# Attention's keys, queries and values fetched from ScalarE's instruction stream, keys in six pieces, values stored by head group

## The chip, the core and the metric

The kernel runs on one core of a Trainium2 chip. The core has five engines with an instruction stream each: TensorE (PE, matmuls; its weight loads are listed apart as PEld), VectorE (DVE), ScalarE (ACT), GpSimd (POOL) and SyncE (SP), which here issues nearly all transfers. All transfers, whoever issues them, run on the core's 16 DMA engines. The metric is the time of one execution on the device in microseconds (us); lower is better.

## What is computed

The reference applies two blocks to x of 2 x 2048 x 512 numbers. The change touches the attention of the first block only:

```python
h = _ada_ln(x, cond, Wln1, bln1)
q = heads(h @ Wq + bq)          # B=2, H=16 heads of HD=32, L=2048
k = heads(h @ Wk + bk)
v = heads(h @ Wv + bv)
scores = einsum('bhqd,bhkd->bhqk', q, k) / sqrt(HD)
attn = softmax(scores, axis=-1)
out = einsum('bhqk,bhkd->bhqd', attn, v)
x = x + out @ Wo + bo
# then LayerNorm and a 512-2048-512 MLP, then a graph attention over 20 nodes
```

## The kernel before

The program is written by hand, engine by engine, with semaphores; each engine runs its stream in order. It has these stages: queries, keys and values (0 to 376 us), attention (376 to 2026 us), output projection, MLP, graph attention.

**First stage.** Eight chunks of 512 rows (`ci`), twelve steps each (`j`). Steps 0 to 7 make queries and keys, steps 8 to 11 values. Each result goes to a tile (`st`, `vst`) and from there by SP to internal DRAM: queries and keys to `qk_d`, values to `v_d` as plain rows, [B * S, D] (lines 592 and 597). At chunk 4 SP also loads the first keys into `ks` (`sp_load_k`, L377, three transfers of 1 MB at steps 1, 3 and 5) and the first two query blocks into `qs` (`sp_load_q`, L384, three transfers of 256 KB each, at steps 6 and 7); at step 8 it loads the next chunk of x (L547). The keys need three copies because a product is made of the high and low parts of numbers, and the rows of `ks` and `qs` hold high, low and high part (32 rows each).

**Attention.** A group `w` is one batch and four heads, 8 in all; `w` has four units `v` (512 queries each), 32 in all (`NU`). A unit is eight pairs `f` (two key tiles of 128 each, `kt` 0 to 15). For a pair:
- PE makes eight maxima products (`pe_max`, L359) and eight score products (`pe_scores`, L621) in turn, then the value products of the pair before, four heads of two key tiles (`pe_values`, L633). The maxima run 82 products ahead of the scores, so they need the queries of unit v + 2 from the seventh product of pair 5 of unit v on, and the keys of the next `w` from pair 5 of its third unit on.
- Scores go to three PSUM banks in turn: `pe_scores` n waits for exponential n - 3.
- ACT does one exponential for each score (`act_exp`, L689, tile `pt` of 8 slots), and, once a unit after pair 0, copies the finished values (`act_values`, L695).
- DVE reduces the maxima (`dve_max`, L372).
- The sums over keys are split: GpSimd adds the tiles `kt` 3, 5, 7, 9, 11, 13, 14 itself (`pacc`, L777), and issues accumulating transfers of 1 MB for `kt` 1, 2, 4, 6, 8, 10, 12 into two accumulators (`accd`, L767 the first two, L763 the others), where each waits for the last one on its own accumulator: 1, 4, 8, 12 on one and 2, 6, 10 on the other. After pair 0 of the next unit PE adds up all parts with products by ones (`pe_sums`, L639, 32 products), the last eight of them over the accumulator that `kt` 12 finishes.
- SP, once a unit: folds the sums (L792), stores and loads their reciprocals (L798, L805), stores two rows made of the maxima (L337, `qs<-nmr`) and the finished values (L812); GpSimd multiplies by the reciprocals (L749) after `kt` 9.

SP's place for the fetches: the queries of v + 2 at pair 2 behind the folding of the sums; the keys of the next `w` in three pieces of 1 MB, at pair 6 of the first unit and pairs 4 and 7 of the second; the values of the next `w` (1 MB, rows of 512 bytes) at pair 7 of the third. All stand in one stream with the other transfers, so the times at which they are issued follow from those:

```python
if v + NCH - c < NU and (c, f) in ((0, 6), (1, 4), (1, 7)):
    sp.wait_ge(s_pad, 5)
    if w >= 2:
        sp.wait_ge(s_sc, 256 * (w - 1))
    sp_load_k(w, ((0, 6), (1, 4), (1, 7)).index((c, f)))
```

`s_pad` 5 is given when GpSimd has filled the spare rows of the second key buffer (L525, L528), at the start of the attention.

Of the kernel before, what the change touches and what calls it, by code (L numbers as in the profile page):

```python
# [7 lines left out]
F32 = mybir.dt.float32  # L8
# [6 lines left out]
B, S, D = 2, 2048, 512  # L15
H, HD = 16, 32
# [7 lines left out]
CH = 512  # L24
NCH = S // CH
# [4 lines left out]
NU = B * (H // 4) * NCH  # L30
# [117 lines left out]
def program(nc, a):  # L148
    pe, act, dve, pool, sp = nc.tensor, nc.scalar, nc.vector, nc.gpsimd, nc.sync
    qk_d = nc.dram_tensor("qk_d", [B, 4, D, S], F32, kind="Internal").ap()  # L150
    v_d = nc.dram_tensor("v_d", [B * S, D], F32, kind="Internal").ap()
    ao_d = nc.dram_tensor("ao_d", [NT, 128, D], F32, kind="Internal").ap()
    r_d = nc.dram_tensor("r_d", [2, 4, CH], F32, kind="Internal").ap()
    x2_d = nc.dram_tensor("x2_d", [B * S, D], F32, kind="Internal").ap()
# [10 lines left out]
    with ExitStack() as ctx:  # L165
# [34 lines left out]
        qsb = take("qs", [128, 3, 4, CH], F32R)  # L200
# [83 lines left out]
        def pe_early(step):  # L284

            if step == 64:
                return
            if step == 65:
                pe.wait_ge(s_nm, 1)
                pe.transpose(ps[0:16, 6, 0:128], nm[:, :], ident[:, :]).then_inc(s_nt, 1)  # L290
                return
            u = step - step // 64 * 2
            v, n = divmod(u, 64)
            hq, kc = divmod(n, 4)
            if n == 0:
                pe.wait_ge(s_qd[v], 48)
                pe.wait_ge(s_kd[0], 48)
            if u == 64:
                pe.wait_ge(s_nh, 2)
            if u >= 2:  # L300
                pe.wait_ge(s_mr, u - 1)
            pe.matmul(ps[:, 6 + u % 2, :], qsb[0:96, v, hq // 4, 128 * (hq % 4):128 * (hq % 4) + 128],
                      ksb[0][0:96, hq // 4, CH * kc:CH * kc + CH], start=True, stop=True).then_inc(s_mm, 1)
# [47 lines left out]
        def pe_max(u):  # L351
            v, n = divmod(u, 64)
            w = v // NCH
            hq, kc = divmod(n, 4)
            if n == 0:
                pe.wait_ge(s_qd[v % 3], 48 * (v // 3 + 1))
                pe.wait_ge(s_kd[w % 2], 48 * (w // 2 + 1))
            pe_bank_free(("max", u))
            pe.matmul(ps[:, ring.bank["max", u], :], qsb[0:96, v % 3, hq // 4, 128 * (hq % 4):128 * (hq % 4) + 128],  # L359
                      ksb[w % 2][0:96, hq // 4, CH * kc:CH * kc + CH], start=True, stop=True).then_inc(s_mm, 1)  # L360
# [11 lines left out]
            dve.tensor_reduce(nmp[:, n // 4, n % 4:n % 4 + 1], ps[:, ring.bank["max", u], :], AX.X, ALU.max,  # L372
                              negate=True).then_inc(s_mr, 1)

        def sp_load_k(w, r):
            b, f, part = w // 4, 128 * (w % 4), (2, 3, 2)[r]
            sp.dma_start(ksb[w % 2][32 * r:32 * r + 32, :, :].bitcast(F32),  # L377
                         qk_d[b, part, f:f + 128, :].rearrange("(h e) s -> e h s", e=HD)).then_inc(s_kd[w % 2], 16)

        def sp_load_q(v):  # L380
            w, qc = divmod(v, NCH)
            b, f = w // 4, 128 * (w % 4)
            for r, part in enumerate((0, 0, 1)):
                sp.dma_start(qsb[32 * r:32 * r + 32, v % 3, :, :].bitcast(F32),  # L384
                             qk_d[b, part, f:f + 128, CH * qc:CH * qc + CH].rearrange("(h e) s -> e h s", e=HD)
                             ).then_inc(s_qd[v % 3], 16)

# [162 lines left out]
        def sp_qkv():  # L550
            step = 0
            sp_load_ss(0, (0, 2))
            sp.dma_start(ident[:, :], a["c_ident"]).then_inc(s_ident, 16)
            sp_load_x(0)
            sp_load_ss(0, (1, 3))
            for i, name in enumerate(("Wq", "Wk", "Wv")):
                if i == 1:
                    sp.dma_start(bvB[:, :], row("bv")).then_inc(s_bias, 16)
                    sp.dma_start(bqk[:, 0, :], a["bqc"]).then_inc(s_bias, 16)
                    sp.dma_start(bqk[:, 1, :], a["bkc"]).then_inc(s_bias, 16)  # L560
                if i == 2:
                    sp_load_x(1)
                for k in range(NK):
                    if i:
                        sp.wait_ge(s_wlo, 4 * i + k - 3)
                    sp.dma_start(wtmp[:, k, :], ktiles(a[name])[:, k, :]).then_inc(s_wt[k], 16)
            sp_load_ss(1, (0, 2, 1, 3))
            for ci in range(NC8):
                b, c = divmod(ci, NCH)
                for j in range(12):  # L570
                    if ci == NCH and j == 1:
                        for r in range(8):
                            sp.wait_ge(s_qst[r], 128)
                        sp.wait_ge(s_pad, 3)
                    if ci == NCH and j in (1, 3, 5):
                        sp_load_k(0, j // 2)
                    if ci == NCH and j in (6, 7):
                        sp_load_q(j - 6)
                    if ci == NCH + 2 and j == 0:
                        sp_load_q(2)  # L580
                    if j == 8 and ci + 2 < NC8:
                        sp_load_x(ci + 2)
                    if with_maxima(ci, j):
                        step += 3
                        if step - 3 <= 65 < step:
                            sp_row(0)
                    if j < 8:
                        u = 8 * ci + j
                        for x, done in ((0, s_qh), (1, s_ql)):
                            r = 2 * (u % 4) + x  # L590
                            sp.wait_ge(done, u + 1)
                            sp.dma_start(qk_d[b, 2 * (j // 4) + x, 128 * (j % 4):128 * (j % 4) + 128,
                                              CH * c:CH * c + CH], st[:, r, :].bitcast(F32)).then_inc(s_qst[r], 16)
                    else:
                        rows0 = CH * ci + 128 * (j - 8)
                        sp.wait_ge(s_vev, 4 * ci + j - 7)
                        sp.dma_start(v_d[rows0:rows0 + 128, :], vst[:, j - 8, :]).then_inc(s_vst[j - 8], 16)

# [12 lines left out]
        def pe_scores(g, hh):  # L611
            v, kt = divmod(g, 16)
            w, n = v // NCH, 4 * g + hh
            if kt == 0 and hh == 0:
                pe.wait_ge(s_qd[v % 3], 48 * (v // 3 + 1))
                pe.wait_ge(s_kd[w % 2], 48 * (w // 2 + 1))
# [80 lines left out]
        def act_attention():  # L697
            qkv_over(act)
            for p in range(NGRP // 2):
                v, f = divmod(p, 8)  # L700
                for n in range(8):
                    act_exp(2 * p + n // 4, n % 4)
                if f == 0 and v:
                    act_values(v - 1)
                if v == NU - 2 and f % 2:
                    k = f // 2
                    act_split(12 + k, wo[:, 0, k, :], wtmpo[:, k, :], s_wo, 16)
            act_values(NU - 1)
# [70 lines left out]
                    pool_values(v - 1)  # L779
            pool_values(NU - 1)  # L780

        def sp_load_v(w):
            b, f = w // 4, 128 * (w % 4)
            sp.dma_start(vq[:, w % 2, :, :],
                         v_d[S * b:S * b + S, f:f + 128].rearrange("(t p) e -> p t e", p=128)).then_inc(s_vq[w % 2], 16)

        def sp_fold_sums(v):

# [25 lines left out]

        def sp_attention():
            qkv_over(sp)
            sp_load_v(0)
            for p in range(NGRP // 2):
                v, f = divmod(p, 8)
                w, c = v // NCH + 1, v % NCH  # L820
                if f == 1 and v:
                    sp_fold_sums(v - 1)
                if f == 2 and v >= 1 and v + 2 < NU:
                    sp.wait_ge(s_sc, 64 * v)
                    sp_load_q(v + 2)
                if f == 3 and v:
                    sp_store_recip(v - 1)
                    sp_load_recip(v - 1)
# [1 line left out]
                    sp_row(v + 1)  # L830
                if f == 7 and v:
                    sp_store_ao(v - 1)
                if v + NCH - c < NU and (c, f) in ((0, 6), (1, 4), (1, 7)):
                    sp.wait_ge(s_pad, 5)
                    if w >= 2:
                        sp.wait_ge(s_sc, 256 * (w - 1))
                    sp_load_k(w, ((0, 6), (1, 4), (1, 7)).index((c, f)))
                if v + NCH - c < NU and (c, f) == (2, 7):
                    if w >= 2:
                        sp.wait_ge(s_pv, 64 * (w - 1))  # L840
                    sp_load_v(w)
# [1044 lines left out]
```

## Time and profile before

| | us |
|---|---|
| median of 3 runs | 3331.78 (3321.52 to 3339.5) |
| the profiled execution | 3324.57 |
| its span | 3323.3 |
| PE busy | 3203.7 (96%) |
| DVE busy | 2072.6 (62%) |
| POOL busy | 1471.1 (44%) |
| ACT busy | 1394.6 (42%) |
| attention, of the span | 376 to 2026 |

Busy times leave out the issuing of transfers, so ACT's 42% and SP's nothing are computing alone. The span is the profiler's, from the first to the last instruction; 1.3 us lie around it. The 16 DMA engines were 60 to 90% busy over the attention, with a mean of 187 GB/s there.

### The profile page before, as it was taken

The numbers are of one execution on the slowest core, as the hardware profiler recorded it, in microseconds if no ns is written. First come the engines' busy times: TensorE is split into PE (matmuls) and PEld (weight loads), VectorE is DVE, ScalarE is ACT, GpSimd is POOL, SyncE is SP. The second block draws the span as 40 slices with busy tenths as digits, with TensorE's granted clock in tenths as the row PEclk, the third lists the DMA queues.
The fourth block names the chain that finished last, engine by engine and source line by source line (L and its number), as shares of the span: only waits on it lengthen the run. The fifth ranks groups of instructions, "written<-read, shape, count | busy, mean of one in ns | idle before, by whom it ended". The sixth has DMA issues, their size and how long they took to land.

```text
span 3323.3 us, 44389 instructions
## 1 busy us (share of the span) xinstructions
PE 3203.7 (96%) x16890; PEld 2185.3 (66%) x16890; DVE 2072.6 (62%) x3524; ACT 1394.6 (42%) x2707; POOL 1471.1 (44%) x665
## 2 busy tenths in 40 slices
PE   8799999999999999999999996899999999999999
PEld 7677655555555555555555533678888888778888
DVE  4647778778788787887878753833333333226766
ACT  2121466666666666666666663311111111112322
POOL 0200478768777777787777865400000000002222
PEclk9899999999999999999999998999999999999999
DMA  5474588888979888798797857801111111311221
GB/s 196 147 220 138 146 202 186 190 193 187 210 175 204 194 179 203 180 203 194 175 197 186 180 135 205 288 19 39 38 39 39 38 38 40 102 34 64 73 77 58
DMA packets 186171, 466.22 MB, mean 140 GB/s; under 512 B 27196, under 2 KB 69308, under 8 KB 154215
## 3 DMA queue, kind: packets, MB, share of 16 engines
q0 software_dynamic: 32256, 234.90, 31.7%
q1 hardware_dynamic: 153703, 228.49, 23.2%
q8 instruction: 133, 2.18, 0.3%
q14 instruction: 79, 0.65, 0.1%
HBM read 151.90 MB, written 75.76 MB: 69 GB/s over the span
## 4 chain that ended last, share of the span: by engine, by line
PE 84%; DMA 8%; DVE 4%; issue 1%; ACT 1%; POOL 1%; SPq 0%; DVEq 0%; POOLq 0%; ACTq 0%
PE ps L359 13%; PE ps L621 13%; PE ps L633 12%; PE ps L1075 11%; PE ps L1064 11%; DMA accd<-pt 5%; PE ps L433 4%; PE ps L1598 3%; PE ps L639 3%; PE ps L1611 3%; PE ps L437 2%; PE ps L1632 1%; PE ps L937 1%; PE ps L1427 1%; ACT pt L689 1%
## 5 line engine op out<-in xcount | busy, mean ns | idle before, releaser
L372 DVE TENSOR_REDUCE nmp<-ps 128x1 f32<-128x512 f32 x1966 | 1202.2, 682 | 168.7 <-PE ps L359 167.2
L689 ACT ACTIVATE pt<-ps 128x512 f32<-128x512 f32 x2048 | 1034.5, 627 | 564.1 <-PE ps L621 563.6
L777 POOL TENSOR_TENSOR pacc<-pacc,pt 128x2048 f32<-128x2048 f32 x192 | 909.9, 4739 | 46.9 <-ACT pt L689 41.9
L621 PE MATMUL ps<-qs,ks 128*128 128x512 f32 x2048 | 824.6, 405 | 5.4 <-issue 3.2
L359 PE MATMUL ps<-ks,qs 96*128 96x512 f32 x1966 | 812.1, 413 | 8.7 <-DVE nmp L372 5.4
L359 PEld LDWEIGHTS ps<-ks,qs 96*128 96x128 f32 x1966 | 377.8, 192 | 277.3 <-DVE nmp L372 167.4
L633 PE MATMUL ps<-pt,vq 128*32 128x512 f32 x4096 | 495.6, 602 | 0.0
L621 PEld LDWEIGHTS ps<-qs,ks 128*128 128x128 f32 x2048 | 394.2, 193 | 106.2 <-ACT pt L689 25.0
L1064 PE MATMUL ps<-hpb,w 128*128 128x512 f32 x1536 | 380.3, 397 | 3.3 <-DMA x_d<-x 3.3
L1075 PE MATMUL ps<-w,gp 128*128 128x512 f32 x1536 | 380.5, 396 | 2.8 <-DVE gp L1208 2.8
L1075 PEld LDWEIGHTS ps<-w,gp 128*128 128x128 f32 x1536 | 289.4, 189 | 72.0 <-DVE gp L1208 3.2
L1064 PEld LDWEIGHTS ps<-hpb,w 128*128 128x128 f32 x1536 | 287.9, 189 | 69.3 <-issue 5.5
L1206 DVE CAST gp<-g 128x512 fp32r<-128x512 f32 x128 | 63.2, 494 | 406.7 <-ACT g L1198 406.7
L1198 ACT ACTIVATE g<-ps,b1c 128x512 f32<-128x512 f32 x128 | 88.1, 688 | 540.7 <-PE ps L1064 540.7
L633 PEld LDWEIGHTS ps<-pt,vq 128*32 128x32 f32 x4096 | 107.5, 109 | 248.3 <-ACT pt L689 166.2
L1330 POOL TENSOR_TENSOR res<-res,b2B 128x512 f32<-128x512 f32 x32 | 41.1, 1314 | 476.0 <-DMA res<-x_d 476.0
L108 POOL TENSOR_SCALAR ve<-mv 128x4 f32<-128x4 f32 x16 | 3.6, 228 | 411.1 <-DVE mv L103 411.1
L777 POOL TENSOR_TENSOR pacc<-pt 128x2048 f32<-128x2048 f32 x32 | 147.0, 4594 | 36.7 <-ACT pt L689 36.7
L763 POOL DMA_DIRECT2D accd<-pt x160 | 149.5, 935 | 9.2 <-ACT pt L689 8.9
L767 POOL DMA_DIRECT2D accd<-pt x64 | 37.3, 583 | 256.0 <-PE ps L639 189.4
L467 ACT ACTIVATE st<-ps,bqk 128x512 fp32r<-128x512 f32 x64 | 44.0, 688 | 236.3 <-PE ps L433 236.2
L714 DVE COPY accs<-ps 128x512 f32<-128x512 f32 x32 | 22.1, 692 | 191.8 <-PE ps L639 191.8
(169 smaller groups left out, 3166.3 us busy)
## 6 DMA issues: line engine op xcount, KB each, us to landing
accd<-pt POOLq DMA_DIRECT2D x224, 1024.0 KB, 8.8
qk_d<-st SPq DMA_DIRECT2D x128, 256.0 KB, 2.7
ks<-qk_d SPq DMA_DIRECT2D x24, 1024.0 KB, 17.2
qs<-qk_d SPq DMA_DIRECT2D x96, 256.0 KB, 6.7
xina<-in_x SPq DMA_DIRECT2D x8, 1024.0 KB, 6.3
v_d<-vst SPq DMA_DIRECT2D x32, 256.0 KB, 2.3
vq<-v_d SPq DMA_DIRECT2D x8, 1024.0 KB, 13.9
recb<-r_d SPq DMA_DIRECT2D x32, 256.0 KB
```

Source lines behind the costliest of these rows:

```text
L359: pe.matmul(ps[:, ring.bank["max", u], :], qsb[0:96, v % 3, hq // 4, 128 * (hq % 4):128 * (hq % 4) + 128], ksb[w % 2][0:96, hq // 4, CH * ...
L372: dve.tensor_reduce(nmp[:, n // 4, n % 4:n % 4 + 1], ps[:, ring.bank["max", u], :], AX.X, ALU.max, negate=True).then_inc(s_mr, 1)
L433: m = pe.matmul(ps[:, bank, :], w[:, x, k, col:col + 128], hp[:, y, k, :], start=(i == 0 and k == 0), stop=(i == 2 and k == NK - 1))
L621: pe.matmul(ps[:, n % 3, :], ksb[w % 2][:, hh, 128 * kt:128 * kt + 128], qsb[:, v % 3, hh, :], start=True, stop=True).then_inc(s_sc, 1)
L633: m = pe.matmul(ps[32 * hh:32 * hh + 32, 7, :], vq[:, w % 2, kt, 32 * hh:32 * hh + 32], pt[:, g % 8, hh, :], start=(kt == 0), stop=(kt == 15))
L639: m = pe.matmul(ps[32 * hh:32 * hh + 32, bank, :], ones[:, :], src[:, hh, :], start=start, stop=stop)
L689: act.activation(pt[:, g % 8, hh, :], ps[:, n % 3, :], ACT.Exp, scale=SCALE).then_inc(s_exp, 1)
L763: pool.dma_start(accd[:, j % 2, :, :], pt[:, g % 8, :, :], accum_op=ALU.add).then_inc(s_dma[j % 2], 16)
L777: pool.tensor_tensor(pacc[:, :, :], first, pt[:, g % 8, :, :], ALU.add).then_inc(s_add, 1)
L1064: m = pe.matmul(ps[:, 4 + r, :], w1[:, f // 4, x, k, 128 * (f % 4):128 * (f % 4) + 128], hp[:, y, k, :], start=(i == 0 and k == 0), stop=( ...
L1075: m = pe.matmul(ps[:, t, :], gp[:, q % 2, x, 128 * t:128 * t + 128], w2[:, f // 4, y, f % 4, :], start=(i == 0 and f == 0), stop=(i == 2 a ...
L1598: pe.matmul(ps[:, 1 + d, 0:320], xp[:, j, x, 128 * k:128 * k + 128], gg[b][:, y, k, 320 * d:320 * d + 320], start=(i == 0 and k == 0), sto ...
```

## The change

It does four things.
- The fetches of keys, queries and values in the attention are issued by ACT, which has a DMA queue of its own, and no longer by SP. They stand behind the eight exponentials of a pair: queries (three transfers in a row) at pair 2, key pieces at pairs 1, 3 and 4 of the first and the second unit of each `w`, values at pair 4 of the third.
- Keys come in six pieces of 512 KB (two heads each) in place of three of 1 MB; the six of the first group are still SP's, two in a row at each of the three old places.
- `v_d` is laid out as [group w, partition p, key tile t, 128]. A fetch of values is then one contiguous 8 KB run a partition, and a store of values is four runs of 512 bytes a partition.
- The counts waited for on `s_kd` go from 48 to 96.

```diff
-    v_d = nc.dram_tensor("v_d", [B * S, D], F32, kind="Internal").ap()
+    v_d = nc.dram_tensor("v_d", [4 * B, 128, S // 128, 128], F32, kind="Internal").ap()
...
-                pe.wait_ge(s_kd[w % 2], 48 * (w // 2 + 1))
+                pe.wait_ge(s_kd[w % 2], 96 * (w // 2 + 1))
...
-        def sp_load_k(w, r):
-            b, f, part = w // 4, 128 * (w % 4), (2, 3, 2)[r]
-            sp.dma_start(ksb[w % 2][32 * r:32 * r + 32, :, :].bitcast(F32),
-                         qk_d[b, part, f:f + 128, :].rearrange("(h e) s -> e h s", e=HD)).then_inc(s_kd[w % 2], 16)
+        def load_k(eng, w, r, half):
+            b, f, part = w // 4, 128 * (w % 4) + 64 * half, (2, 3, 2)[r]
+            eng.dma_start(ksb[w % 2][32 * r:32 * r + 32, 2 * half:2 * half + 2, :].bitcast(F32),
+                          qk_d[b, part, f:f + 64, :].rearrange("(h e) s -> e h s", e=HD)).then_inc(s_kd[w % 2], 16)
...
                     if ci == NCH and j in (1, 3, 5):
-                        sp_load_k(0, j // 2)
+                        load_k(sp, 0, j // 2, 0)
+                        load_k(sp, 0, j // 2, 1)
...
-                        sp.dma_start(v_d[rows0:rows0 + 128, :], vst[:, j - 8, :]).then_inc(s_vst[j - 8], 16)
+                        sp.dma_start(v_d[4 * b:4 * b + 4, :, 4 * c + j - 8, :].rearrange("w p e -> p w e"),
+                                     vst[:, j - 8, :].rearrange("p (w e) -> p w e", w=4)).then_inc(s_vst[j - 8], 16)
...
                 if f == 0 and v:
                     act_values(v - 1)
+                w, c = v // NCH + 1, v % NCH
+                if f == 2 and v >= 1 and v + 2 < NU:
+                    act.wait_ge(s_sc, 64 * v)
+                    load_q(act, v + 2)
+                if w < 2 * NCH and c < 2 and f in (1, 3, 4):
+                    i = 3 * c + (1, 3, 4).index(f)
+                    act.wait_ge(s_pad, 5)
+                    if w >= 2:
+                        act.wait_ge(s_sc, 256 * (w - 1))
+                    load_k(act, w, i // 2, i % 2)
+                if w < 2 * NCH and (c, f) == (2, 4):
+                    if w >= 2:
+                        act.wait_ge(s_pv, 64 * (w - 1))
+                    load_v(act, w)
...
-                if f == 2 and v >= 1 and v + 2 < NU:
-                    sp.wait_ge(s_sc, 64 * v)
-                    sp_load_q(v + 2)
```

ACT's stream over units 3 to 5 of the attention before. `pt` is the exponentials' tile, `accv` the copy of the finished values.

```order
L695 ACTIVATE accv_81<-ps 128x512
L689 ACTIVATE pt_78<-ps 128x512 x64
L695 ACTIVATE accv_81<-ps 128x512
L689 ACTIVATE pt_78<-ps 128x512 x64
L695 ACTIVATE accv_81<-ps 128x512
```

Nothing stands between the exponentials of a unit but that copy. ACT's stream now, from a copy at pair 0 of unit 4 (`w` 2 is fetched) to the end of pair 3 of unit 5. `ks`, `qs` are the keys' and queries' tiles.

```order
L697 ACTIVATE accv_81<-ps 128x512
L691 ACTIVATE pt_78<-ps 128x512 x8
L378 DMA ks0_57<-qk_d 32x2x2048
L691 ACTIVATE pt_78<-ps 128x512 x8
L385 DMA qs_58<-qk_d 32x4x512 x3
L691 ACTIVATE pt_78<-ps 128x512 x8
L378 DMA ks0_57<-qk_d 32x2x2048
L691 ACTIVATE pt_78<-ps 128x512 x8
L378 DMA ks0_57<-qk_d 32x2x2048
L691 ACTIVATE pt_78<-ps 128x512 x32
L697 ACTIVATE accv_81<-ps 128x512
```

What moved: behind the exponentials of pairs 1, 3 and 4 stands one transfer now, behind those of pair 2 stand three in a row, and the exponentials of the next pair stand behind them.

SP's stream before, from the last transfer of one unit over the second unit of a group: sums (`rs`), queries, reciprocals (`r_d`, `recb`), keys, rows (`nmr`), finished values (`ao_d`), keys.

```order
L792 DMA rs_86<-accs_82 128x1x16
L384 DMA qs_58<-qk_d 32x4x512 x3
L798 DMA r_d<-rr_87 128x16
L805 DMA recb_83<-r_d 128x1x512
L377 DMA ks1_76<-qk_d 32x4x2048
L337 DMA qs_58<-nmr_61 1x16x128 x2
L812 DMA ao_d<-aout_84 128x4x128
```

The large fetches (`ks`, `qs`) stand between the small transfers. The same unit now, on SP:

```order
L806 DMA rs_86<-accs_82 128x1x16
L812 DMA r_d<-rr_87 128x16
L819 DMA recb_83<-r_d 128x1x512
L337 DMA qs_58<-nmr_61 1x16x128 x2
L826 DMA ao_d<-aout_84 128x4x128
```

What moved: nothing large is left on SP; the queries no longer stand ahead of the reciprocals, nor a key piece behind them.

## Rows read from the trace of the kernel before

**Rows 1.** The page: busy time of PE, instructions; then PE's waits, attention.

```profile
PE 3203.7 (96%) x16890; PEld 2185.3 (66%) x16890; DVE 2072.6 (62%) x3524; ACT 1394.6 (42%) x2707; POOL 1471.1 (44%) x665
...
PE ps L639 <- DMA accd<-pt: 20.2, 7, 4.4
```

**Rows 2.** The chain: start, length, what (products by ones, once a unit).

```profile
428.58 3.43 PE ps L639 x32
...
738.18 3.43 PE ps L639 x32
837.90 3.43 PE ps L639 x32
938.89 3.43 PE ps L639 x32
...
1809.71 3.43 PE ps L639 x32
```

**Rows 3.** Stretches: window, length, PE, PEld, DVE, ACT, POOL (count), clock, DMA, GB/s.

```profile
633.50:688.30 54.80, 52.51 (x317) 28.49 (x305) 40.54 (x69) 33.40 (x66) 38.80 (x15) 1.00 0.90 198
...
738.20:788.07 49.87, 49.87 (x293) 27.88 (x289) 40.54 (x69) 32.80 (x65) 38.81 (x15) 1.00 0.77 175
```

**Rows 4.** The chain in unit 5.

```profile
657.95 15.84 DMA accd<-pt
...
674.32 14.78 DMA accd<-pt
```

**Rows 5.** Timeline (start, length, engine, line, [idle before <-releaser]), unit 5's fetches and sums.

```profile
655.95 1.24 SPq L377 DMA_DIRECT2D ks<-qk_d  x1
...
668.74 0.45 SPq L377 DMA_DIRECT2D ks<-qk_d  x1
...
689.15 1.06 PE L639 MATMUL ps<-accd,ones 128*32 128x512 f32 x8 [3.14 <-DMA accd<-pt]
```

**Rows 6.** Timeline, pairs 2 and 3 of unit 5: exponentials, fourth and last score.

```profile
649.29 4.03 ACT L689 ACTIVATE pt<-ps 128x512 f32<-128x512 f32 x8 [1.80 <-PE ps L621]
...
650.26 0.40 PE L621 MATMUL ps<-qs,ks 128*128 128x512 f32 x1
...
652.13 0.40 PE L621 MATMUL ps<-qs,ks 128*128 128x512 f32 x1
```

**Rows 7.** SP's issues of queries (two in the first stage, two in attention) and values.

```profile
220.53 1.51 SPq L384 DMA_DIRECT2D qs<-qk_d  x3
...
223.73 4.26 SPq L384 DMA_DIRECT2D qs<-qk_d  x3
...
725.00 1.35 SPq L784 DMA_DIRECT2D vq<-v_d  x1
...
1199.15 2.77 SPq L384 DMA_DIRECT2D qs<-qk_d  x3
...
1403.95 3.46 SPq L384 DMA_DIRECT2D qs<-qk_d  x3
```

**Rows 8.** The queries' source line, 600 to 700 us: issue to landing.

```profile
DMA to landing us min/median/max: 6.1/6.9/10.4
```

**Rows 9.** Stretches behind a stop of PE: columns as in rows 3.

```profile
690.00:693.00 3.00, 3.00 (x12) 2.25 (x9) 2.58 (x4) 1.50 (x3) 0.61 (x1) 0.61 0.40 153
...
891.00:894.00 3.00, 2.66 (x19) 1.46 (x16) 1.44 (x3) 0.81 (x2) 0.61 (x1) 1.00 0.00 0
```

**Rows 10.** Timeline, start of the attention: the spare rows' second fill; pair 2's exponentials.

```profile
383.35 6.92 POOL L528 MEMSET ks<- 2x8192 f32 x1
...
388.72 4.03 ACT L689 ACTIVATE pt<-ps 128x512 f32<-128x512 f32 x8 [1.93 <-PE ps L621]
```

**Rows 11.** SP in chunk 4 of the first stage: third key piece, next store.

```profile
217.31 1.13 SPq L377 DMA_DIRECT2D ks<-qk_d  x1
219.32 1.16 SPq L592 DMA_DIRECT2D qk_d<-st  x2
```

**Rows 12.** The chain, chunk 4 of the first stage.

```profile
231.27 14.19 DMA xina<-in_x
```

More of the change, by code:

```diff
@@ L296, in pe_early @@
                 pe.wait_ge(s_qd[v], 48)
-                pe.wait_ge(s_kd[0], 48)
+                pe.wait_ge(s_kd[0], 96)
             if u == 64:
@@ L373, in dve_max, with load_q @@
                               negate=True).then_inc(s_mr, 1)
-        def sp_load_k(w, r):
-            b, f, part = w // 4, 128 * (w % 4), (2, 3, 2)[r]
-            sp.dma_start(ksb[w % 2][32 * r:32 * r + 32, :, :].bitcast(F32),
-                         qk_d[b, part, f:f + 128, :].rearrange("(h e) s -> e h s", e=HD)).then_inc(s_kd[w % 2], 16)
-        def sp_load_q(v):
+        def load_k(eng, w, r, half):
+            b, f, part = w // 4, 128 * (w % 4) + 64 * half, (2, 3, 2)[r]
+            eng.dma_start(ksb[w % 2][32 * r:32 * r + 32, 2 * half:2 * half + 2, :].bitcast(F32),
+                          qk_d[b, part, f:f + 64, :].rearrange("(h e) s -> e h s", e=HD)).then_inc(s_kd[w % 2], 16)
+        def load_q(eng, v):
             w, qc = divmod(v, NCH)
@@ L383, in sp_load_q @@
             for r, part in enumerate((0, 0, 1)):
-                sp.dma_start(qsb[32 * r:32 * r + 32, v % 3, :, :].bitcast(F32),
-                             qk_d[b, part, f:f + 128, CH * qc:CH * qc + CH].rearrange("(h e) s -> e h s", e=HD)
-                             ).then_inc(s_qd[v % 3], 16)
+                eng.dma_start(qsb[32 * r:32 * r + 32, v % 3, :, :].bitcast(F32),
+                              qk_d[b, part, f:f + 128, CH * qc:CH * qc + CH].rearrange("(h e) s -> e h s", e=HD)
+                              ).then_inc(s_qd[v % 3], 16)
         def pe_out_free(nb):
@@ L575, in sp_qkv @@
                     if ci == NCH and j in (1, 3, 5):
-                        sp_load_k(0, j // 2)
+                        load_k(sp, 0, j // 2, 0)
+                        load_k(sp, 0, j // 2, 1)
                     if ci == NCH and j in (6, 7):
-                        sp_load_q(j - 6)
+                        load_q(sp, j - 6)
                     if ci == NCH + 2 and j == 0:
-                        sp_load_q(2)
+                        load_q(sp, 2)
                     if j == 8 and ci + 2 < NC8:
@@ L594, in sp_qkv @@
                     else:
-                        rows0 = CH * ci + 128 * (j - 8)
                         sp.wait_ge(s_vev, 4 * ci + j - 7)
-                        sp.dma_start(v_d[rows0:rows0 + 128, :], vst[:, j - 8, :]).then_inc(s_vst[j - 8], 16)
+                        sp.dma_start(v_d[4 * b:4 * b + 4, :, 4 * c + j - 8, :].rearrange("w p e -> p w e"),
+                                     vst[:, j - 8, :].rearrange("p (w e) -> p w e", w=4)).then_inc(s_vst[j - 8], 16)
         def qkv_over(eng):
@@ L615, in pe_scores @@
                 pe.wait_ge(s_qd[v % 3], 48 * (v // 3 + 1))
-                pe.wait_ge(s_kd[w % 2], 48 * (w // 2 + 1))
+                pe.wait_ge(s_kd[w % 2], 96 * (w // 2 + 1))
                 pe.wait_ge(s_md, 32 * (v + 1))
@@ L780, in pool_attention, with load_v @@
             pool_values(NU - 1)
[L782 to L785, printed above, removed]
+        def load_v(eng, w):
+            eng.dma_start(vq[:, w % 2, :, :], v_d[w]).then_inc(s_vq[w % 2], 16)
         def sp_fold_sums(v):
@@ L816, in sp_attention @@
             qkv_over(sp)
-            sp_load_v(0)
+            load_v(sp, 0)
             for p in range(NGRP // 2):
                 v, f = divmod(p, 8)
-                w, c = v // NCH + 1, v % NCH
                 if f == 1 and v:
                     sp_fold_sums(v - 1)
-                if f == 2 and v >= 1 and v + 2 < NU:
-                    sp.wait_ge(s_sc, 64 * v)
-                    sp_load_q(v + 2)
                 if f == 3 and v:
@@ L832, in sp_attention @@
                     sp_store_ao(v - 1)
[L833 to L841, printed above, removed]
                 if f == 4 and v == NU - NCH:
```

## Prediction

> **What bounds the kernel now.** First the page: PE is busy 96% of the span [rows 1], so a gain must come from PE's gaps, slow clock or shorter work, and any new gap on PE is paid in full. The attention holds half the span. There the chain has 32 products by ones once a unit (L639), a mark by which units can be timed. From the second mark to the fourth shown, 738.18 to 837.90, two units pass: 49.86 us each. From unit 1's mark at 428.58 to unit 28's at 1809.71 there are 27 units in 1381.1 us, which at 49.86 would take 1346.2. **34.9 us are lost**, in seven places, one for each group of heads [rows 2]. The stretches show where: the unit beginning at 633.5 took 54.8 us with the DMA engines 0.90 busy, a later one 49.87 at 0.77 [rows 3]. The mechanism is in the chain: the accumulating transfer of `kt` 8 starts at 657.95 and takes 15.84 us, `kt` 12 waits for it, starts at 674.32 and takes 14.78 [rows 4], where an `accd` transfer takes 8.8 us in the median of the page. Beside them run the second and the third key piece, issued at 655.95 and 668.74; PE stops for 3.14 us ahead of the last products by ones at 689.15 [rows 5]. PE waited there for `accd` 7 times, 20.2 us in all [rows 1]; the rest of the 34.9 is the clock after a stop: granted 0.61 in 690 to 693, that is partly at 1.2 GHz instead of 2.4, where a stop of under 1 us ahead of 891 left it at 1.00 [rows 9].
>
> **The key pieces move: the stops go.** ACT issues at the end of a pair's exponentials. In unit 5 these end at 641.7 (pair 1), 653.3 (pair 3), 659.1 (pair 4), in steps of 5.8 us around the 649.29 of rows 6. So the last 512 KB start near 659 instead of 1 MB at 668.74. `kt` 8 still meets about 0.7 of the 1 MB it met before, and I keep its landing at 14 to 16 us, that is 672 to 674. `kt` 12 then meets no keys; at 8.8 us it lands at 681 to 683, and PE needs it at 689.15 - 3.14 = 686.0. Margin 3 to 5 us. The group with the smallest loss, 838 to 939, lost 938.89 - 837.90 - 2 x 49.86 = 1.3 us [rows 2]; I leave 0.9 in each of seven, 6.3. **Gain 28.6**; ends 0 (stops stay) and 34.9. The first unit of a group now has three half pieces too, in place of one at its end; its `kt` 12 is as free of keys, so I take nothing for it.
>
> The Trainium skill (DMA: Bandwidth & Descriptors, "Issuing engines are not separate DMA queues") says that starting transfers from several engines saves only the sequencer's issue time, since all run on the same 16 DMA engines. By it a second queue relieves nothing. The trace agrees so far: `accd`, from GpSimd's queue, and `ks`, from SP's, slow each other. My sum therefore takes the gain from the time of the issue alone.
>
> **The queries move to ACT: a new gap on PE.** For each v from 1 to 29, three issues stand between the exponentials of pairs 2 and 3. ACT's idle time there is 1.80 us, from 647.49 to 649.29 [rows 6]. On SP in the attention three such issues took 2.77 to 3.46 us [rows 7], 3.1 in the middle. So the next exponential starts 3.1 - 1.8 = 1.3 us late. PE makes three scores without it; the fourth started at 650.26 and needs exponential one, which ended at 649.29 + 0.6 = 649.9. The eighth, at 652.13, needs exponential five; exponentials follow each other every (4.03 - 0.60) / 7 = 0.49 us, so it ended at 651.85: 0.28 us of slack. PE loses 1.3 - 0.28 = 1.0 us, and 29 x 1.0 = **29 us**. Cover there is none: values, maxima and sums follow on PE in order. The stop is of the length that left the clock at 1.00 [rows 9].
> No row shows an issue by ACT, so this is bounded. From below: three issues took 1.51 us at 220.53, behind a key piece still in flight [rows 7], under the 1.8 us of idle time; then the cost is 0. From above: 4.26 us at 223.73, with more in the queue; in the 14 of the 29 units that have a key piece 5.8 us ahead that is 14 x (4.26 - 3.1) = 16 more, 45. I take the attention's own figure because load and neighbours are the same there.
>
> **Single issues.** 42 key pieces and 7 fetches of values, one at a time: the longest such rows are 1.24 and 1.35 us [rows 5, 7], under 1.8 us of idle ACT: nothing. Values come earlier and as 8 KB runs; no stop of PE follows the one at 725, the two units behind it are the regular ones of rows 2: nothing.
>
> **One wait.** At pair 1 of unit 0 ACT waits for the spare rows' fill, which ends at 383.35 + 6.92 = 390.27. The exponentials of pair 1 end at 388.72 - 1.93 = 386.8 and the next ones start at 388.72 [rows 10]. Behind the wait stands the whole ACT stream: with 0.5 us for the issue it resumes at 390.8, 2.1 late, less 0.28: **1.8 us** on PE, up to 4 if the clock falls too.
>
> **First stage.** SP has three more issues and stores of 512-byte runs. The longest key issue took 1.13 us, and 0.88 us pass idle between its end and the next store at 219.32 [rows 11]: a second one overruns by some 0.3. SP then issues the x of chunk 6, whose transfer of 14.19 us is on the chain [rows 12], beside the value stores. I take **1 us**; ends 0 and 4.
>
> **When queries land.** They are issued later than before, and in order behind a key piece. The third starts at about 649.3 (647.5, 0.5 for the first, 1.3 for the second), and PE wants it at the seventh maxima product of pair 5, about 663. Landing took 6.1 to 10.4 us [rows 8], 660 at worst: nothing.
>
> **Sum**, against the profiled execution of 3324.57 (span 3323.3): 3324.6 + 29 + 1.8 + 1 - 28.6 = 3327.8, rounded to **3328**. That execution is 7 us under the median of the three runs, 3331.78, and inside their range of 3321.5 to 3339.5; I give the number on its base.
>
> **The rivals.**
> *B, the issues on ACT are short.* Three of them take 1.5 us as at 220.53 and are hidden; the sum loses its 29: 3299, with the stops gone entirely 3292. For it: that row, and that ACT's queue is often empty. Against: SP's queue was empty too at the queries' place, and the three took 2.8 to 3.5 us in each unit. The Trainium skill (same page, the table of sequencer times in its part on fast descriptor generation) gives 512 sequencer cycles for a transfer's issue on earlier generations, and 1.2 GHz for the sequencer's clock (Advanced Engine Details and Errata, "Clock Domains"): an estimate of 0.43 us each, 1.3 for three. By that rule it would be this rival. The trace agrees for the first of a row of issues and not for three.
> *C, slower: the stops stay.* Place: the last products by ones of each group's second unit. The six pieces and the queries all fall between 641 and 666 in it, `kt` 8 takes as long or longer, and `kt` 12, bound to it, comes late. It decides from where `kt` 12 lands after 686 in unit 5's terms, that is from a `kt` 8 that lands after about 677. Price: the gain of 28.6 falls away while the 30.8 of the issues stand: 3324.6 + 29 + 1.8 + 1 = 3356.
> *D, slower: the clock falls with each gap.* If ACT's issues make the stop of PE 2 us or more, it meets what stands behind 690: nine products at 0.43 us instead of 0.235, 1.8 us more. 29 x 1.8 = 52 on top of 3328 is 3380.
>
> **How the numbers follow.** Forecast (gain and cost cancel) 0.43, its own range 3312 to 3344; B 0.32; C 0.15; D 0.10. Half a per cent is 16.6 us, about what a measurement of this kernel can tell from no change. B is faster by more, the forecast is inside, C and D are slower: 0.32, 0.43, 0.25; I move 0.01 from slower to faster for a C in which some of the stops go: 0.33, 0.43, 0.24. Range: from 3297, which leaves out the best part of B (0.07), to 3362, which leaves out D: 0.8 held.
>
> **What would show it.** In the new profile: a row of three `qs` issues on ACT's queue, over 1.8 us or under it, and ahead of pair 3's exponentials no idle time released by PE; on PE waits of L621 for the exponentials, 29 of about 1 us (B: none; D: 2 us with a clock below 1.00). On L639 waits for `accd` near zero and marks 50.9 apart in all units (C: 55 in each second unit). `kt` 12 landing in 9 us and `ks` transfers of 512 KB. A wait of PE near 389 of 2 us. The forecast is wrong first by the length of ACT's issues, which nothing here shows, and then by whether `kt` 8 lets `kt` 12 start in time.

## The result and the profile after

The changed kernel takes 3454.3 us (3447.6 to 3462.3) where the kernel before takes 3330.2 on the same chip: a ratio of 1.037, with a 95% interval of 1.034 to 1.041. It is 124 us slower; the forecast was 3328 and the range ended at 3362. The profiled execution has a span of 3460.7 us, 137 more than before. The attention, from 376 to 2151 us, has 124 of them; the other 13 lie behind it, in stages that the change does not touch, and the medians don't show them.

The page of the changed kernel: busy times, and the chain that ended last by engine and line.

```profile
PE 3249.3 (94%) x16890; PEld 2194.2 (63%) x16890; DVE 2071.0 (60%) x3524; ACT 1392.9 (40%) x2707; POOL 1468.4 (42%) x665
...
PE 65%; POOL 16%; issue 8%; ACT 4%; DVE 4%; DMA 2%; ACTq 1%; SPq 0%; POOLq 0%; DVEq 0%
POOL pacc L793 14%; PE ps L1076 10%; PE ps L1065 10%; PE ps L623 7%; PE ps L359 7%; PE ps L635 6%; PE ps L434 4%; ACT pt L691 4%; PE ps L1599 3%; PE ps L641 3%; PE ps L1612 2%; PE ps L438 2%; PE ps L1633 1%; PE ps L1428 1%; DMA ao<-ao_d 1%
```

GpSimd, which does no more than before, now holds 16% of the chain. Waits of PE, then of GpSimd, in the attention of the changed kernel (us in total, times, longest):

```profile
PE ps L641 <- POOL pacc L793: 108.5, 26, 6.8
...
PE ps L623 <- ACT pt L691: 7.0, 16, 1.4
...
PE ps L641 <- DMA accd<-pt: 1.9, 2, 1.5
...
POOL aout L765 <- DMA recb<-r_d: 228.6, 28, 11.4
```

The waits for `accd` that the prediction started from, 20.2 us [rows 1], are down to 1.9. In their place PE waits 108.5 us at the same products for GpSimd's additions `pacc`; and GpSimd waits 228.6 us for `recb`, the reciprocals, ahead of `aout`, its product by them. The same line of the kernel before, from 376 to 2026 us:

```profile
POOL aout L749 <- DMA recb<-r_d: 40.9, 29, 4.9
```

One unit shows the whole loop. Timelines of the changed kernel, units 4 to 5 (start, length, engine, line): VectorE, SyncE, GpSimd, TensorE.

```profile
656.73 0.69 DVE L730 COPY accs<-ps 128x512 f32<-128x512 f32 x1 [10.63 <-PE ps L641]
...
657.45 0.60 SPq L806 DMA_DIRECT2D rs<-accs  x1
...
667.74 0.24 DVE L736 RECIPROCAL rr<-rs 128x16 f32<-128x16 f32 x1
...
668.00 0.32 SPq L812 DMA_DIRECT2D r_d<-rr  x1
676.65 0.57 SPq L819 DMA_DIRECT2D recb<-r_d  x1
...
693.53 1.28 POOL L765 TENSOR_TENSOR aout<-accv,recb 128x512 f32<-128x512 f32 x1 [9.46 <-DMA recb<-r_d]
694.76 0.88 POOL L779 DMA_DIRECT2D accd<-pt  x1
...
700.54 9.78 POOL L793 TENSOR_TENSOR pacc<-pacc,pt 128x2048 f32<-128x2048 f32 x2
...
710.38 1.53 PE L641 MATMUL ps<-pacc,ones 128*32 128x512 f32 x8 [4.95 <-POOL pacc L793]
711.66 1.95 PE L641 MATMUL ps<-accd,ones 128*32 128x512 f32 x8
...
713.66 0.69 DVE L730 COPY accs<-ps 128x512 f32<-128x512 f32 x1 [10.44 <-PE ps L641]
```

The same places in a regular unit of the kernel before, unit 7.

```profile
741.68 0.69 DVE L714 COPY accs<-ps 128x512 f32<-128x512 f32 x1 [3.95 <-PE ps L639]
...
752.66 0.25 DVE L720 RECIPROCAL rr<-rs 128x16 f32<-128x16 f32 x1
...
752.93 0.34 SPq L798 DMA_DIRECT2D r_d<-rr  x1
759.38 0.57 SPq L805 DMA_DIRECT2D recb<-r_d  x1
...
769.36 1.28 POOL L749 TENSOR_TENSOR aout<-accv,recb 128x512 f32<-128x512 f32 x1 [0.92 <-DMA recb<-r_d]
...
776.37 9.93 POOL L777 TENSOR_TENSOR pacc<-pacc,pt 128x2048 f32<-128x2048 f32 x2
```

Read both from the copy of the sums. Up to the store of the reciprocals they are equal (11.3 us). Then the store takes 8.7 us in place of 6.4, and from the issue of the load to `aout` pass 16.9 us in place of 10.0: `aout` starts 36.8 us after the copy, not 27.7. (Unit 7 has no key pieces beside it. Unit 5 of the kernel before has two, at other moments: there 11.4 us pass from the issue of the load to `aout`, and `aout` starts 29.6 us after the copy.) Behind `aout` GpSimd's stream has no gap: its last two additions end 16.8 us after it in one kernel and 16.9 in the other. PE takes `pacc` 2 us ahead of the next copy, so in a period of 49.9 us `aout` may start at most 49.9 - 2 - 16.9 = 31 us after the copy. Before, it used 27.7 of them and was waiting for `recb` even so. At 36.8 it is 5 to 6 us late, PE stops for 4.95 us, and the next sums and so the next reciprocals start late as well. The period is 36.8 + 16.8 + 3.3 = 56.9 us. Such a stop has a second price, the clock (stretches of the changed kernel, columns as in rows 3):

```profile
711.00:714.00 3.00, 3.00 (x17) 0.70 (x9) 0.34 (x1) 0.00 (x0) 0.00 (x0) 0.50 0.02 5
714.00:717.00 3.00, 3.00 (x14) 2.39 (x14) 2.98 (x6) 2.38 (x5) 0.62 (x2) 0.96 0.59 229
```

After the 4.95 us TensorE was granted 0.50 of its clock, 1.2 GHz, and the last eight products took 1.95 us, where they take 1.04 in unit 7 of the kernel before. Of the unit's 7.0 us over 49.9, 5 are the wait, and the other 2 go with the slow clock. From the first unit's copy to the one 28 units later it is 1557.4 us in the changed kernel and 1435.1 before: 4.4 us a unit, 122 us, which is the loss. It is not even. Units beside keys or values take 56 to 59 us with one exception, the fourth of a group, which has only the queries beside it, 50 to 53.

And this is what was expected to cost: ScalarE's issues. Timeline of ACT and its queue, pairs 2 and 3 of unit 5 of the changed kernel.

```profile
663.18 3.54 ACT L691 ACTIVATE pt<-ps 128x512 f32<-128x512 f32 x7 [1.80 <-PE ps L623]
666.50 0.31 ACTq L385 DMA_DIRECT2D qs<-qk_d  x1
666.53 0.67 ACT L691 ACTIVATE pt<-ps 128x512 f32<-128x512 f32 x1
666.84 2.72 ACTq L385 DMA_DIRECT2D qs<-qk_d  x2
669.68 3.54 ACT L691 ACTIVATE pt<-ps 128x512 f32<-128x512 f32 x7 [2.48 <-PE ps L623]
```

The first issue takes 0.31 us and starts with the last exponential, not behind its end. The idle time grows from 1.80 to 2.48 us, most of which PE's slack takes up. Over the attention PE waited 7.0 us in 16 places for exponentials, where it waited 2.2 before.

### The profile page after: what moved, and what is told of

Read it like the earlier page. It is cut to its first block, busy times and chain, and to the rows that moved or that the text cites. A ratio compares the mean times of both kernels' runs of the same rounds, so it can differ in the third digit from the quotient of the medians.

```text
span 3460.7 us, 44431 instructions
## 1 busy us (share of the span) xinstructions
PE 3249.3 (94%) x16890; PEld 2194.2 (63%) x16890; DVE 2071.0 (60%) x3524; ACT 1392.9 (40%) x2707; POOL 1468.4 (42%) x665
## 4 chain that ended last, share of the span: by engine, by line
PE 65%; POOL 16%; issue 8%; ACT 4%; DVE 4%; DMA 2%; ACTq 1%; SPq 0%; POOLq 0%; DVEq 0%
POOL pacc L793 14%; PE ps L1076 10%; PE ps L1065 10%; PE ps L623 7%; PE ps L359 7%; PE ps L635 6%; PE ps L434 4%; ACT pt L691 4%; PE ps L1599 3%; PE ps L641 3%; PE ps L1612 2%; PE ps L438 2%; PE ps L1633 1%; PE ps L1428 1%; DMA ao<-ao_d 1%
## 5 line engine op out<-in xcount | busy, mean ns | idle before, releaser
L779 POOL DMA_DIRECT2D accd<-pt x160 | 149.0, 931 | 8.5 <-ACT pt L691 6.9
L641 PE MATMUL ps<-pacc,ones 128*32 128x512 f32 x256 | 50.1, 867 | 108.5 <-POOL pacc L793 108.5
L765 POOL TENSOR_TENSOR aout<-accv,recb 128x512 f32<-128x512 f32 x32 | 41.2, 1286 | 240.0 <-DMA recb<-r_d 240.0
```

The costliest lines, as they stand in the source:

```text
L641: m = pe.matmul(ps[32 * hh:32 * hh + 32, bank, :], ones[:, :], src[:, hh, :], start=start, stop=stop)
L779: pool.dma_start(accd[:, j % 2, :, :], pt[:, g % 8, :, :], accum_op=ALU.add).then_inc(s_dma[j % 2], 16)
```

## Experiments

The theory after the two traces (R): the fetches now run in the window in which the reciprocals are stored and loaded, 11 to 30 us after the copy; they slow these two small transfers, and through GpSimd's stream the lateness reaches PE. Rivals: ScalarE's issues; a queue of its own as such; the smaller pieces and the new layout of values. All ratios are to the kernel before on the same chip, with 95% intervals.

### aout behind tile 12

```diff
-                if kt == 9 and v:
+                if kt == 12 and v:
                     pool_values(v - 1)
```

> The changed kernel, with GpSimd's product by the reciprocals (aout) behind key tile 12 of a unit in place of 9; all transfers are issued where the changed kernel issues them. Theory R (the reciprocals come late and, through GpSimd's in-order stream, hold up its own additions, for which PE waits): the late transfer, some 17 us to the start of aout, stays, but nothing of the additions stands behind it. PE's waits for pacc fall from 108 us to under 15, units take some 50 us, and the kernel takes 3290 to 3320 us, below the kernel before. Rival (ScalarE's issues or slower transfers of any kind are the cause): the time stays within 20 us of 3454.

Measured: 3450 us, 1.030 (1.027 to 1.034). The total spoke for the rival, the waits of PE for the theory, and a new one had come:

```profile
PE ps L623 <- issue: 98.5, 20, 7.6
...
PE ps L641 <- POOL pacc L793: 9.2, 10, 1.5
...
702.00 0.65 PE L623 MATMUL ps<-qs,ks 128*128 128x512 f32 x1 [4.80 <-issue]
```

The waits for `pacc` are gone, 9.2 us are left. PE now stops at a unit's first score. The profile names no releaser, but that score waits for the rows made of the maxima (`qs<-nmr`). SP issued their second transfer at 686.6 us, and it took 15.2 us to land, that is until 701.8; PE went on at 702.0. The longest such landing from 500 to 1800 us was 18.1 us, against 9.1 before. The load of the reciprocals had become slower still: 23.6 us in this unit, with tile 10's accumulating transfer now issued beside it instead of behind it. So a second consumer hangs on SP's small transfers, and the first had hidden it.

### aout behind tile 12, and the load in four transfers

```diff
-            sp.dma_start(recb[:, :], r_d[v % 2].unsqueeze(1).to_broadcast([4, 32, CH])).then_inc(s_recb, 16)
+            for h in range(4):
+                sp.dma_start(recb[32 * h:32 * h + 32, :],
+                             r_d[v % 2, h:h + 1].to_broadcast([32, CH])).then_inc(s_recb, 16)
...
-                if kt == 9 and v:
+                if kt == 12 and v:
```

The counts waited for on the load go from 16 to 64 with it (not shown). The load alone in four, everything else as changed:

> The changed kernel with the load of the reciprocals cut in four transfers, one for each head, 32 rows of 2 KB each from one row of DRAM, in place of one whose source has four rows of 2 KB, each repeated 32 times. Same bytes, same moment. Theory S (the load is slow because its shape keeps it on few of the 16 DMA engines, where each of its packets waits its turn behind key packets): aout starts 8 us after the issue or sooner, in place of 17, PE's waits for pacc fall from 108 us to under 20, total 3300 to 3345. Theory B (the bytes of all transfers in those 15 us are too many, whatever the shape): the load still takes over 14 us, total over 3420.

Measured: 3399 us, 1.019 (1.017 to 1.022). The load takes 14 us from its first issue, in place of 17, although its four issues stretch over 2.9 us of it in the median and 4.4 at most; PE waits 58.3 us for `pacc`, where it waited 108.5. The shape carries about half of the loss, and neither theory's total was met. The Trainium skill (DMA: Bandwidth & Descriptors, "Rules for kernel authors") says that a leading broadcast of c copies or any outermost size under 16 confines a transfer to at most c DMA engines; here the source led with 4. No view here counts the engines of a transfer, but the load's time moved the way this rule would have it.

Both together:

> The changed kernel with the load of the reciprocals in four transfers and aout behind key tile 12. In a_aout12 PE's waits for pacc fell to 9 us, but it stopped 98 us for the rows made of the maxima (qs<-nmr), which SP issues behind the load of the reciprocals and which landed 6 to 15 us later. Theory R2 (two consumers hang on SP's small transfers, the reciprocals through GpSimd and the rows through PE's first score of a unit; each alone holds the unit at some 57 us): the load now takes 14 us in place of 25, rows land in time, aout holds nothing up, and the kernel takes 3300 to 3345. If the time stays over 3390, a third thing holds the units.

Measured: 3319 us, 0.994 (0.992 to 0.996), and in the waits of PE:

```profile
PE ps L641 <- POOL pacc L793: 7.2, 9, 1.5
...
PE ps L623 <- issue: 4.6, 2, 3.5
```

This is the changed kernel with every fetch where the change put it, on ScalarE's queue, still beside the reciprocals: the store still takes 8.7 us and `aout` starts 36 us after the copy. But nothing that PE needs hangs on it, since the additions stand ahead and the rows land in 4.2 to 7.2 us (from 500 to 1800 us). All 124 us are back and 19 more. PE's waits for `accd` are gone too: the transfer of tile 12 takes 8.4 to 9.5 us in the second unit of each group, where it took 12 to 16 before. The theory is shown by this run: the loss was the two consumers behind SP's small transfers.

### The same moments on SP's queue

All fetches of the attention are taken out of ScalarE's stream (not shown). In SP's stream, where `sp_key` first waits for the exponentials of its pair:

```diff
+                if f == 1 and keys:
+                    sp_key(1)
+                if f == 2 and v >= 1 and v + 2 < NU:
+                    sp.wait_ge(s_exp, 8 * p + 8)
+                    sp.wait_ge(s_sc, 64 * v)
+                    load_q(sp, v + 2)
                 if f == 3 and v:
                     sp_store_recip(v - 1)
+                if f == 3 and keys:
+                    sp_key(3)
+                if f == 3 and v:
                     sp_load_recip(v - 1)
+                if f == 4 and keys:
+                    sp_key(4)
+                if w < 2 * NCH and (c, f) == (2, 4):
+                    sp.wait_ge(s_exp, 8 * p + 8)
...
+                    load_v(sp, w)
```

> The changed kernel, with queries, key pieces and values issued by SP again, but at the same moments: SP waits for the exponentials of the same pair before each of them. Between them stand the two reciprocal transfers. Theory Q (a queue of their own gives the fetches a share beside SP's queue, so that the reciprocals no longer go ahead of or apart from them): the load of the reciprocals takes its old 9 to 11 us, units some 50, total 3300 to 3340. Theory T (it is the moment, whichever queue): the load takes 15 us or more as in the changed kernel, total 3430 or more.

Measured: 3447 us, 1.031 (1.028 to 1.033). SP's queue in it:

```profile
666.30 2.83 SPq L385 DMA_DIRECT2D qs<-qk_d  x3
669.23 1.16 SPq L798 DMA_DIRECT2D r_d<-rr  x1
...
677.68 0.57 SPq L805 DMA_DIRECT2D recb<-r_d  x1
...
691.11 1.29 POOL L751 TENSOR_TENSOR aout<-accv,recb 128x512 f32<-128x512 f32 x1 [8.57 <-DMA recb<-r_d]
```

The load takes 13.4 us here, 3.5 less than on separate queues, but the store starts 2.7 us later, behind the queries' issues, and `aout` again starts 36 us after the copy. Theory T's total was met, its load of 15 us or more was not. Whose queue it is makes little difference; the moment does. The Trainium skill (DMA: Bandwidth & Descriptors, "Issuing engines are not separate DMA queues") says that transfers issued by any engine run on the same 16 DMA engines, and that issuing from several saves only the time of the issues. The measurement agrees: 1.031 against 1.037.

### Other moments on ScalarE's queue

```diff
-                if f == 2 and v >= 1 and v + 2 < NU:
+                if f == 0 and v >= 1 and v + 2 < NU:
...
-                if w < 2 * NCH and c < 2 and f in (1, 3, 4):
-                    i = 3 * c + (1, 3, 4).index(f)
+                if w < 2 * NCH and c < 2 and f in (5, 6, 7):
+                    i = 3 * c + (5, 6, 7).index(f)
...
-                if w < 2 * NCH and (c, f) == (2, 4):
+                if w < 2 * NCH and (c, f) == (2, 6):
```

> The changed kernel, still on ScalarE's queue, with queries behind pair 0 in place of 2, key pieces behind pairs 5, 6 and 7 in place of 1, 3 and 4, values behind pair 6 in place of 4 of the third unit. Theory R and T: the reciprocals move between pairs 2 and 5 beside nothing but accumulating transfers, their load takes 10 us, and PE's waits for pacc go; but keys run beside tile 12's accumulating transfer, so that stops of 3 us on accd come back in up to two units of each group: 3290 to 3345. If a queue of their own is itself what costs: 3400 or more.

Measured: 3318.5 us, 0.992 (0.990 to 0.994): faster than the kernel before. The store takes 5.2 to 6.3 us and the load 10 to 12, `aout` starts 27 to 29 us after the copy, the period is 49.9 in most units. PE waits 9.7 us for `accd` and 0.8 for `pacc`. Keys beside tile 12 cost less than I had expected.

### Which of the fetches

> The changed kernel with the key pieces alone moved, behind pairs 5, 6 and 7 in place of 1, 3 and 4; queries stay behind pair 2, values behind pair 4. If the key pieces beside the load are the cause, all units but those with a fetch of values (7 of 32) fall to 50 or 52 us, and the kernel takes 3345 to 3375. If it is the queries, 3430 or more stays.

Measured: 3395 us, 1.018 (1.015 to 1.022), above what was expected: with the keys away, the load still takes 13 to 16 us in many units without a fetch of values, and PE still waits 60.8 us for `pacc`. So the queries have a share of their own. The units beside a fetch of values stay at 55 to 57 us, as expected.

> The changed kernel with the queries fetched by SP at their old place, behind the fold of the sums, some 9 us earlier; keys and values as changed. Keys as the cause: the load still takes 15 us in the units with keys, total 3410 to 3450. Queries as the cause (they stand beside the store of the reciprocals and the start of their load): 3300 to 3350.

Measured: 3418 us, 1.025 (1.023 to 1.028), inside what was expected with keys as the cause. Units beside keys have a period of 57 to 59 us; in nearly all of them the store now takes 12 to 15 us, and the load 12 to 15 as well. Units beside a fetch of values have 50 to 51, so values cost next to nothing by themselves. With the queries on ScalarE's queue beside them the same units have 55 to 57 (a_keys_late, and the changed kernel).

> The kernel before with the queries alone on ScalarE, behind pair 2; keys in three pieces and values as before, on SP. Keys as the cause of the loss: the store of the reciprocals takes 2 us longer as it does now beside queries, units in which aout had waited 0.3 to 2.9 us wait 2 us more, total 3330 to 3360. Queries as the cause: 3400 or more. Three issues in a row on ScalarE cost PE under 0.3 us a unit, as in the changed kernel.

```diff
+                if f == 2 and v >= 1 and v + 2 < NU:
+                    act.wait_ge(s_sc, 64 * v)
+                    load_q(act, v + 2)
...
-                if f == 2 and v >= 1 and v + 2 < NU:
-                    sp.wait_ge(s_sc, 64 * v)
-                    sp_load_q(v + 2)
```

Measured: 3366 us, 1.008 (1.005 to 1.012), a little over what was expected. The store takes 8.2 to 9.5 us in nearly all units, the load 12 to 14 in many. PE waits 30.5 us for `pacc` and 26.0 for `accd`, and 8.1 for exponentials, under 0.3 us a unit as expected.

Queries alone cost 0.8%, keys and values alone 2.5%, all together 3.7%, which the intervals don't tell from the sum.

### Layout and pieces alone

> The kernel before with the parts of the change that are not the move: values stored by head group and fetched as 8 KB runs, keys in six pieces, two in a row where one stood; all issued by SP at the old places. Theory: layout and pieces are worth nothing, the move is all of the loss: 3315 to 3345, ratio 0.995 to 1.005. A rival that blames the smaller pieces or the stores of 512 bytes expects over 3350.

Measured: 3340.9 us, 1.001 (0.999 to 1.003), with PE's wait for `accd` back at 21.1 us. Pieces and layout are worth nothing that can be measured.

### Versions beyond

> The kernel before, with aout behind key tile 12 in place of 9 and nothing else. There aout waits 0.3 to 4.9 us a unit, 41 in all, and PE hardly ever for pacc. Tile 10's accumulating transfer starts up to 5 us earlier in the units with keys, tile 12's hangs on tile 8's and doesn't. Expected 3310 to 3332: the same to 0.5% less. It tells how much of what a_aout12 gains belongs to the place of aout alone.

Measured: 3322.7 us, 0.993 (0.991 to 0.996). One number in the kernel before gains 0.7%. What it removed are the stops on `accd`, the 20.2 us of the prediction's first paragraph: none is left among PE's waits, and 10.8 us for `pacc` stand in their place. Unit 5 shows how (GpSimd, SyncE):

```profile
674.37 0.87 POOL L763 DMA_DIRECT2D accd<-pt  x1 [4.51 <-ACT pt L689]
...
676.59 0.38 SPq L812 DMA_DIRECT2D ao_d<-aout  x1
677.07 1.30 SPq L377 DMA_DIRECT2D ks<-qk_d  x1
```

In SP's stream the third key piece stands behind the store of the finished values, which waits for `aout`. With `aout` later it is issued at 677.07, not 668.74 [rows 5], and the transfer of tile 12 takes 9.5 us, not 14.8. In the second units of all later groups it takes 8.6 to 9.7 us, where it took 12 to 16. So the stops have two cures: the last key piece earlier, as in the change, or later, as here. That this is what b_aout12 gains is read from the two traces; no run moves that piece alone.

> a_times (queries behind pair 0, keys 5 to 7, values 6, on ScalarE's queue; 0.992 of the kernel before) with aout behind key tile 12, which alone was worth 0.993 on the kernel before. There PE still waited 9.7 us for accd and some 5 for a score. If the two gains come from different stops: 3295 to 3312, ratio 0.985 to 0.990. If both took away the same lateness of GpSimd: 3315 to 3320.

Measured: 3317.7 us, 0.994 (0.992 to 0.997): as a_times. The second expectation's number was met. In a_times nothing on PE hung on the place of `aout` any more: it waits 9.7 us for `accd` and 0.8 for `pacc` there, 8.8 and 0.8 here.

> a_times with the load of the reciprocals in four transfers. If the shape is slow only beside the fetches, the load takes 9 us in place of 10 to 12 and the time stays at 3310 to 3320; if few DMA engines are what it costs always, it takes 6 to 7 us, aout no longer waits (38 us now), and the time falls to 3300 or below.

Measured: 3299.3 us, **0.989** (0.986 to 0.991), the fastest of all. GpSimd in it, in a unit:

```profile
710.82 1.29 POOL L765 TENSOR_TENSOR aout<-accv,recb 128x512 f32<-128x512 f32 x1
...
717.89 9.87 POOL L793 TENSOR_TENSOR pacc<-pacc,pt 128x2048 f32<-128x2048 f32 x2
...
734.54 0.60 POOL L783 DMA_DIRECT2D accd<-pt  x1 [6.79 <-PE ps L641]
```

`aout` follows the addition before it at once, with no idle time, 26.7 us after the copy in each of the first 29 units, and the period is 49.8 to 50.0 in all of them. The last of the load's four pieces lands 7.3 us after the first issue in the median, where the load took 10 to 12. PE waits 0.7 us for `accd` and 0.8 for `pacc`. The second of the two expectations holds: the shape cost something always. It cost its neighbour too: the transfer of tile 8, which runs beside the load, takes 7.3 us in the median of the units without keys and values, where it took 11.0 in a_times. Tile 12, which waits for it, starts 33.1 us after the copy in the second units, not 34 to 36, and so its 13 to 14 us beside keys no longer stop PE.

## Why the prediction was wrong

**What bounds the kernel, and the stops on accd:** right. The accumulating transfers of tiles 8 and 12 were held up by key pieces, and with the last piece earlier the wait went from 20.2 to 1.9 us. The changed kernel can't show this by itself, since its tile 12 starts late behind `aout`; a_recb4_aout12 does (8.4 to 9.5 us for tile 12), and b_aout12, where the last piece is later instead. The gain of 28.6 did not show because another wait took its place. With that wait cured and the fetches left where the change put them, 19 us of gain show (a_recb4_aout12); b_aout12 gets 18 from the same stops without the change. The 39 us of a_times_recb4 come with the fetches at other moments.

**The queries move to ACT:** the term was mis-sized. I took 3.1 us for three issues, beginning at the end of the last exponential, and 1.0 us of PE for each of 29. The first takes 0.31 us beside the last exponential, three take 1.33 us in the median of the 29 rows (1.3 to 4.2), and all the waits of PE for exponentials are 7.0 us, not 29. SP's figure did not carry over to ScalarE: at the same moments three issues take 2.8 us in the median on SP (a_spq). In this, rival B was right. The rule that I had set beside it, an estimate of 0.43 us an issue and 1.3 for three from the Trainium skill (DMA: Bandwidth & Descriptors, the table of sequencer times), was the nearer one. The bound from above counted 14 units with a key piece ahead of the queries; there are 13, as unit 0 fetches no queries.

**One wait:** right. ACT resumed at 390.29, and PE stopped before its score at 390.94 (changed kernel):

```profile
389.90 0.35 ACTq L378 DMA_DIRECT2D ks<-qk_d  x1
390.29 4.03 ACT L691 ACTIVATE pt<-ps 128x512 f32<-128x512 f32 x8 [3.82 <-POOL ks L529]
...
390.94 0.50 PE L623 MATMUL ps<-qs,ks 128*128 128x512 f32 x1 [1.42 <-ACT pt L691]
```

1.42 us against 1.8 predicted.

**Values:** nothing was taken for them. By themselves they cost next to nothing (a_q_sp), but together with the queries they made units of 56 us.

**First stage:** 1 us predicted. SP issued the x of chunk 6 at 230.33, 0.9 us earlier than before, and the attention did not start later: nothing.

**The step that failed** is one that the sum didn't have. "My sum therefore takes the gain from the time of the issue alone" was applied to one neighbour of the moved transfers, the accumulating ones. The fetches had been moved out of the time of tile 12 and into that of the reciprocals' store and load, and for these I wrote no term; without a reason I had put them at nothing. They were the whole loss: 108.5 us of waits for `pacc`, and the clock behind them. Of each transfer that is moved, one must ask what it now runs beside. The trace of before told it: GpSimd's `aout` waited for `recb` in nearly every unit, mostly by 0.3 to 1.4 us and by 2.7 to 4.9 in the units in which keys are in flight (40.9 in all), a wait small enough to overlook, but one that says that the chain of small transfers sets when `aout` starts, with 31 - 27.7 = 3 us to go until PE would feel it. It got 9 us. None of my rivals had this mechanism; C named the right place, the products by ones (L639), and the wrong party, `accd` for `pacc`.

**The range:** it was drawn from the bounds of terms that were there. A missing term has no bound.

## What to carry to other kernels

- A transfer that moves in time changes its neighbours. Before moving a large fetch, list the small transfers in whose window it will fall, and follow each to the engine that waits for it and to what stands behind the waiter in its stream. A wait of 0.3 us that returns every period means that chain has no slack of its own.
- A product of low urgency placed in the middle of an in-order stream (`aout` ahead of three additions) makes its inputs as urgent as what stands behind it; putting it behind tile 12 took PE's waits for `pacc` from 108.5 us to 9.2 in the changed kernel. It also moved what stood behind it in another stream: the 0.7% that it gained in the kernel before goes, by the traces, with a key piece issued 8 us later.
- Where a small transfer is slow under load, look at its shape before its size: the same 256 KB in four transfers of 32 rows gave back half of a 3.7% loss.

## What the runs showed of the hardware

- Issuing a transfer from ScalarE took 0.31 to 0.35 us for each of 49 single ones and overlapped the last exponential. Three in a row took 1.33 us in the median of 29 and 4.2 at most; from SP at the same moments 2.8 in the median (a_spq).
- A load of 256 KB went from 10.0 us to 16.9 beside fetches of 512 KB pieces from another queue, and in one case to 23.6 beside another accumulating transfer as well. The `accd` transfers of 1 MB kept their median of 8.8 us, but not each of them: in the units beside keys that of tile 6 went from 8.3 to 15.4 us in the median, those of tiles 10 and 12 from 10.5 and 13.6 to 7.6 and 8.1. PE waited for none of them but 1.9 us. Why the load suffers was tested for its shape only.
- The same 256 KB loaded in four transfers of 32 rows landed in 7.3 us in the median, where the one took 10 to 12 to its consumer, and the 1 MB transfer beside it went from 11.0 to 7.3 us (a_times to a_times_recb4, the latter in units without keys and values).
- A stop of TensorE of 4.95 us was followed by a granted clock of 0.50 over the next 3 us; stops of 7 us a unit all through the attention left its mean there at 0.96, against 0.99 before.
